# Odd feed-forward blocks take their low half from GpSimd, through a second relu copy by ScalarE

## What is computed

```python
x = x + jnp.tanh(g_xattn[0]) * _L0_xattn_ref(_layernorm(x), ctx, ctx, Wq, bq, Wk, bk, Wv, bv, Wo, bo)
x = x + jnp.tanh(g_ffn[0]) * _L0_ffn_ref(_layernorm(x), W1, b1, A1, B1, R1, W2, b2, A2, B2, R2)

# attention: 16 heads of 16, rotary positions with scale on q and k, softmax over the 154 rows
# feed-forward: both layers are
def _mole(x, W, b, A, Bm, Rw):          # 3 experts of rank 8
    gates = softmax(x @ Rw)
    base = x @ W + b
    z = einsum('bsd,edr->ebsr', x, A)
    zg = z * gates
    return base + (1/8) * einsum('ebsr,erh->bsh', zg, Bm)
h = relu(_mole(x, W1, ...))             # 256 -> 1024
return _mole(h, W2, ...)                # 1024 -> 256
```

## Time and profile before

| | |
|---|---|
| median of 3 runs | 569.35 us (567.44 to 569.93) |
| the profiled execution | 570.09 us, its span 568.3 us |
| mean granted TensorE clock | 0.953 |
| TensorE matmul busy | 505.9 us, 89% of the span |
| VectorE busy | 397.6 us, 70% |
| ScalarE busy | 208.7 us, 37% |
| GpSimd busy | 64.5 us, 11% |

### The profile page before, as it was taken

How to read it: one execution, slowest core, us unless ns; L and a number is a source line. 1 busy time by engine, 2 the same in 40 slices (tenths; PEclk the granted TensorE clock), 3 DMA queues, 4 the chain that set the end, 5 groups by cost and what they waited for, 6 DMA issues and landing times.

```text
span 568.3 us, 7827 instructions
## 1 busy us (share of the span) xinstructions
PE 505.9 (89%) x3032; PEld 375.8 (66%) x3032; DVE 397.6 (70%) x920; ACT 208.7 (37%) x341; POOL 64.5 (11%) x113
## 2 busy tenths in 40 slices
PE   2578865999999899999999999999999999999897
PEld 1345354855977387845977487746976497748697
DVE  4757465858879487958888487958887587925543
ACT  3233521363225612463326512463226413451230
POOL 2336002010110102010101002010201010010000
PEclk9965976999999999999999999999999999999898
DMA  8391044011802062112602171114502080200001
GB/s 294 49 226 39 1 81 68 2 50 45 106 0 76 8 114 30 40 49 66 84 0 77 38 99 14 50 39 82 69 1 76 1 112 1 77 1 1 1 38 37
DMA packets 13329, 31.86 MB, mean 56 GB/s; under 512 B 1732, under 2 KB 2572, under 8 KB 13164
## 3 DMA queue, kind: packets, MB, share of 16 engines
q1 hardware_dynamic: 6983, 14.63, 15.2%
q10 hardware_dynamic: 6309, 16.73, 11.0%
HBM read 14.31 MB, written 4.19 MB: 33 GB/s over the span
## 4 chain that ended last, share of the span: by engine, by line
PE 69%; DVE 16%; ACT 6%; DMA 5%; issue 3%; POOL 0%; SPq 0%; DVEq 0%; ACTq 0%
PE psF L1116 13%; PE psF L1164 13%; PE psX L1147 7%; PE psX L1218 5%; ACT probs L548 4%; DMA qT<-probs 4%; DVE max_t L762 4%; PE psX L1049 4%; PE psO L1232 3%; PE psO L1235 3%; PE psX L1032 2%; PE psF L1232 2%; DVE probs L687 2%; PE psF L1122 2%; PE psF L1235 2%
## 5 line engine op out<-in xcount | busy, mean ns | idle before, releaser
L762 DVE TENSOR_REDUCE max_t<-psX 128x4 fp32r<-128x616 f32 x128 | 99.2, 794 | 9.5 <-PE psX L1147 7.9
L548 ACT ACTIVATE probs<-psX 128x1024 f32<-128x1024 f32 x64 | 64.3, 1025 | 51.0 <-PE psX L1218 51.0
L1164 PE MATMUL psF<-w_hi,h_hi 128*128 128x284 f32 (+1 forms) x240 | 72.7, 303 | 0.0
L1147 PE MATMUL psX<-km,qT 96*128 96x308 f32 x256 | 64.7, 342 | 8.2 <-DMA qT<-probs 4.4
L1164 PE MATMUL psF<-w_lo,h_hi 128*128 128x284 f32 (+1 forms) x240 | 70.9, 296 | 0.0
L1164 PE MATMUL psF<-w_hi,h_lo 128*128 128x284 f32 (+1 forms) x240 | 70.8, 295 | 0.0
L1147 PEld LDWEIGHTS psX<-km,qT 96*128 96x128 f32 x256 | 48.2, 206 | 22.9 <-DVE max_t L762 9.7
L464 ACT ACTIVATE h_hi<-psF 128x512 fp32r<-128x512 f32 x59 | 34.3, 593 | 54.5 <-PE psF L1122 54.5
L1164 PEld LDWEIGHTS psF<-w_hi,h_hi 128*128 128x128 f32 x240 | 45.8, 191 | 4.9 <-issue 4.8
L1164 PEld LDWEIGHTS psF<-w_hi,h_lo 128*128 128x128 f32 x240 | 45.9, 191 | 0.1
L1164 PEld LDWEIGHTS psF<-w_lo,h_hi 128*128 128x128 f32 x240 | 45.7, 191 | 0.0
(11 more groups left out here) (175 smaller groups left out, 928.3 us busy)
## 6 DMA issues: line engine op xcount, KB each, us to landing
qT<-probs SPq DMA_DIRECT2D x32, 256.0 KB, 9.8
qT<-probs ACTq DMA_DIRECT2D x16, 256.0 KB, 8.1
x<-in_x_dram ACTq DMA_DIRECT2D x8, 512.0 KB, 3.3
x_ln<-in_x_dram ACTq DMA_DIRECT2D x7, 512.0 KB, 3.2
out_dram<-x ACTq DMA_DIRECT2D x7, 512.0 KB, 2.7
turn<-in_turns_dram SPq DMA_DIRECT2D x2, 512.0 KB, 10.1
heads_t<-in_w_dram SPq DMA_DIRECT2D x1, 1024.0 KB, 8.4
heads_t<-in_w_dram SPq DMA_DIRECT2D x1, 994.0 KB, 14.1
```

Of the source, the lines that this page charges most:

```text
L548: nc.scalar.activation(dst, psX[:, 2 * (i % 2):2 * (i % 2) + 2, :], ACT.Exp).then_inc(sc_exp.sem, 1)
L762: V.tensor_reduce(max_t[:, k, half, :].rearrange("p (h g) -> p g h", h=2)[:, 2 * j:2 * j + 2, :], psX[:, 2 * j:2 * j + 2, 0:2 * S].rearran ...
L1147: ins = mm(psX[:, g % 4, 0:2 * S], qT[0:KS, g, tokens(k)], km[0:KS, g, :, :].rearrange("p h s -> p (h s)"), start=True, stop=True)
L1164: ins = mm(out_bank(d, k)[:, cs], a[:, m, tokens(k)], w[:, m, cs], start=m == 0 and i == 0, stop=m == HT - 1 and i == 2)
```

## The change

For the odd blocks 1, 3, 5 and 7 of all chunks but the last, VectorE no longer forms the low half. ScalarE takes the relu of the same bank a second time, as exact fp32, into the first quarter, second quarter and so on of `heads_t` (named `h_f`, semaphore `w1_f`), and GpSimd subtracts: `h_lo = h_f - h_hi` (`low_blocks`, semaphore `w1_lo_p`). An odd block's bank is free when the second relu is done. VectorE's transposes of the next heads into `heads_t` wait for GpSimd's reads of the quarter that they overwrite. The first layer of the last chunk stays as it was.

```diff
@@ -210,7 +210,8 @@
         wo_ps, x1_s = count("wo_ps", 2), count("x1_s", 2)
         z1_ps, g1_v, g1_e = count("z1_ps", 1), count("g1_v", 9), count("g1_e", 1)
         z1T_ps, z1T_s = count("z1T_ps", 1), count("z1T_s", 1)
-        w1_ps, w1_hi_s, w1_lo_s = count("w1_ps", HT), count("h_hi_s", HT), count("h_lo_s", HT)
+        w1_ps, w1_hi_s = count("w1_ps", HT), count("h_hi_s", HT)
+        w1_lo_v, w1_lo_p, w1_f = (count(n, len(POOLED)) for n in ("h_lo_v", "h_lo_p", "h_f"))
         w2_ps = count("w2_ps", TT)
         g2_c, g2_v, g2_e = count("g2_c", TT), count("g2_v", 16), count("g2_e", 2)
         z2T_ps, z2T_s = count("z2T_ps", 2), count("z2T_s", 2)
@@ -248,6 +249,8 @@
                 return dict(out=lo, in0=staged[n][64:LR, :], in1=hi[64:LR, :].bitcast(F32), op=ALU.subtract)
             return dict(out=lo, in0=staged[n], in1=hi.bitcast(F32), op=ALU.subtract)
 
+        h_f = heads_t[:, :, :, :].rearrange("p a b c -> p a (b c)")
+
         block = stack.enter_context(nc.Block())
 
 
@@ -329,6 +332,13 @@
                 nc.gpsimd.tensor_tensor(ln_b[:, which, :], ln_n[:, which, :], ln_r[:, which, :],
                                         ALU.mult).then_inc(out_s.sem, 1)
 
+            def low_blocks(d):
+
+                for i, m in enumerate(POOLED):
+                    pool.wait_ge(w1_f.sem, w1_f.at(d, i + 1))
+                    nc.gpsimd.tensor_tensor(h_lo[:, m, :], h_f[:, i, :], h_hi[:, m, :].bitcast(F32),
+                                            ALU.subtract).then_inc(w1_lo_p.sem, 1)
+
             def residual_base(b, u):
 
                 pool.wait_ge(x1_loaded[u].sem, x1_loaded[u].at(b))
@@ -356,6 +366,8 @@
                 if first:
                     stage_low("w2a")
                     stage_low("w2b")
+                else:
+                    low_blocks(c - 1)
                 residual_base(b, u)
 
             rstd(0, ln1_agg, ln1_eps, ln1_rstd, 0)
@@ -462,6 +474,11 @@
 
                 act.wait_ge(w1_ps.sem, w1_ps.at(d, m + 1))
                 nc.scalar.activation(h_hi[:, m, :], hidden_bank(d, m), ACT.Relu).then_inc(w1_hi_s.sem, 1)
+                if m in POOLED and d is not LAST:
+                    i = POOLED.index(m)
+                    if i == 0:
+                        act.wait_ge(o_lo.sem, o_lo.at(d))
+                    nc.scalar.activation(h_f[:, i, :], hidden_bank(d, m), ACT.Relu).then_inc(w1_f.sem, 1)
 
             def maxima_copy(c):
 
@@ -754,7 +771,7 @@
                 dve.wait_ge(w1_hi_s.sem, w1_hi_s.at(d, m + 1))
                 V.scalar_tensor_tensor(out=h_lo[:, m, :], in0=hidden_bank(d, m), scalar=0.0,
                                        in1=h_hi[:, m, :].bitcast(F32), op0=ALU.max,
-                                       op1=ALU.subtract).then_inc(w1_lo_s.sem, 1)
+                                       op1=ALU.subtract).then_inc(w1_lo_v.sem, 1)
 
             def reduce_max(c, i):
                 half, k, j = i // 8, i % 8 // 2, i % 2
@@ -785,6 +802,8 @@
             def head_blocks(c, g):
 
                 dve.wait_ge(pv_ps.sem, pv_ps.at(c, g + 1))
+                if c:
+                    dve.wait_ge(w1_lo_p.sem, w1_lo_p.at(c - 1, g + 1))
                 V.transpose(heads_t[:, g, :, :].rearrange("p c r -> p (c r)"), pv_bank(g)).then_inc(pv_t.sem, 1)
 
             def head_norm(c, f2):
@@ -897,7 +916,8 @@
                     for m in range(HT):
                         if m < HT - 1:
                             reduce_max(c, 2 * m + 2)
-                        h_low(d, m)
+                        if m not in POOLED:
+                            h_low(d, m)
                         if m < HT - 1:
                             reduce_max(c, 2 * m + 3)
 
@@ -1010,7 +1030,7 @@
 
                 pe.wait_ge(ctx_loaded.sem, ctx_loaded.at(b))
                 if src is ctx_sb:
-                    pe.wait_ge(w1_lo_s.sem, w1_lo_s.at(2 * b - 2))
+                    block_taken(2 * b - 2, 7)
                 for f in range(FT):
                     nc.tensor.transpose(psF[:, 2, S * f:S * f + P], src[:, 0, P * f:P * f + P], ident)
                     ins = nc.tensor.transpose(psF[:, 2, S * f + P:S * f + S], src[0:SR, 1, P * f:P * f + P],
@@ -1096,6 +1116,15 @@
                     ins = nc.tensor.transpose(o_ps[:, k].bitcast(F32R), zs[:, k, :], ident_r[:, :])
                 ins.then_inc(z1T_ps.sem, 1)
 
+            def block_taken(d, m):
+
+                done = w1_f if m in POOLED else w1_lo_v
+                pe.wait_ge(done.sem, done.at(d, m // 2 + 1))
+
+            def lows_done(d):
+                pe.wait_ge(w1_lo_v.sem, w1_lo_v.at(d))
+                pe.wait_ge(w1_lo_p.sem, w1_lo_p.at(d))
+
             def hidden_main(d, m, second=False, parts=(0, 1)):
 
                 if d is LAST:
@@ -1104,10 +1133,10 @@
                     elif m == 6:
                         pe.wait_ge(g1_v.sem, g1_v.at(d, 1))
                     elif m == 7:
-                        pe.wait_ge(w1_lo_s.sem, w1_lo_s.at(d, 1))
+                        pe.wait_ge(w1_lo_v.sem, w1_lo_v.at(d, 1))
                 elif parts[0] == 0:
                     if m >= 3:
-                        pe.wait_ge(w1_lo_s.sem, w1_lo_s.at(d, m - 2))
+                        block_taken(d, m - 3)
                     elif not second:
                         pe.wait_ge(y_out.sem, y_out.at(d - 1, m + 2))
                 ops = [(a, w, f) for a, w in ((xT_hi, w1_hi), (xT_lo, w1_hi), (xT_hi, w1_lo)) for f in range(FT)]
@@ -1152,14 +1181,14 @@
 
                 if k == 0 and d is not LAST:
                     pe.wait_ge(w1_hi_s.sem, w1_hi_s.at(d))
-                    pe.wait_ge(w1_lo_s.sem, w1_lo_s.at(d))
+                    lows_done(d)
                 if k == 3 and m0 == 0 and d is not LAST and d is not LAST - 1:
                     pe.wait_ge(y_out.sem, y_out.at(d, 1))
                 cs = slice(0, E if k == 3 and d is LAST else W2N)
                 for m in range(m0, m1):
                     if k == 0 and d is LAST:
                         pe.wait_ge(w1_hi_s.sem, w1_hi_s.at(d, m + 1))
-                        pe.wait_ge(w1_lo_s.sem, w1_lo_s.at(d, max(m + 1, 2)))
+                        pe.wait_ge(w1_lo_v.sem, w1_lo_v.at(d, max(m + 1, 2)))
                     for i, (a, w) in enumerate(((h_hi, w2_hi), (h_lo, w2_hi), (h_hi, w2_lo))):
                         ins = mm(out_bank(d, k)[:, cs], a[:, m, tokens(k)], w[:, m, cs],
                                  start=m == 0 and i == 0, stop=m == HT - 1 and i == 2)
@@ -1305,7 +1334,8 @@
                         max_transposed(c, 1, first)
                     if i == 1 and not last:
                         if not first:
-                            pe.wait_ge(w1_lo_s.sem, w1_lo_s.at(d, 7))
+                            block_taken(d, 5)
+                            block_taken(d, 6)
                         transpose_x(c + 1, psF, ln1_out, xT_ps)
                     if i == 3 and u == 1 and not last:
                         ctx_transposed(b + 1, ctx_sb)
@@ -1377,6 +1407,7 @@
 PV_AFTER = [3, 5, 8, 10]
 PV_SLOT = {3: 0, 5: 1, 8: 2}
 LAST = B * UB - 1
+POOLED = (1, 3, 5, 7)
 QT_ACT = [0, 1, 2, 3, 4, 6]
 F_OF_K = [0, 1, 2, 0]
```

## The result

| | before | after |
|---|---|---|
| median (20 runs each) | 568.58 us (567.23 to 570.71) | 571.22 us (568.08 to 573.90) |
| ratio | | 1.0040, 95% interval 1.0023 to 1.0058 |
| profiled execution, span | 570.09, 568.3 us | 571.22, 569.4 us |

A forecast was written before the change was run, and what follows sets the result against it. TensorE was taken as the bound, with 69% of the chain; gain 0, GpSimd's price 0, and 0.35 us lost in each of six steps gave +2.1 us, median 571.4 us, range 568.5 to 575.0 us.

The forecast's parts named there:

- The forecast: Whole kernel: median of 571.4 us, 0.4% slower, from +2.1 us; given 45%.
- Nothing waits behind the odd low halves: Hidden blocks: removing VectorE's 28 instructions gains 0, at most 3.2 us.
- 0.48 us for the activation, not 0.60: Second relu of block 5, ahead of layer norm: delays relu 6 by 0.48 us; upper bound 0.60, full duration.
- Rival 3: Activation costs more than its spacing, or scores 1 and exponentials add waits: 0.47 to 0.59 us a step; chance 25%.
- 0.35 us a step: End of hidden blocks, steps 1 to 6: late relu 6 moves h_low(6) from 307.20 to 307.55, reduction 15 following.
- rival 2: Score part: reduction 15's delay is caught up there, no change, 569.4 us; chance 20%.
- Step 7 as before: Last step: no layer norm between relu 5 and relu 6, so relu 6 isn't late; nothing lost or won.
- GpSimd's price of 0: GpSimd's 28 added subtractions, 1.28 us each, 35.8 us in all, delay no reader: 0 us.
- The cover of 0.3 us in the last step: Last step: block 7's subtraction ends near 495.8, its reader starts at 496.09; covered by 0.3 us.
- The odd steps' first exponential: Odd steps: DMA issues behind two added activations delay the first exponential by some 0.4 us; third exponential still covered.
- the sum: Whole kernel: 6 x 0.35 = +2.1 us, on the profiled 570.09 us giving 572.2.
- VectorE's busy time: Whole kernel: falls by 19 us, from 28 removed instructions of 0.68 us.

The follow-up runs named there:

- block 5's copy alone: Kernel before plus one unread second relu of block 5 on ScalarE after relu 5 in steps 1 to 7, with waits for it; ratio 1.0012.
- the even blocks: Changed kernel with blocks 0, 2, 4 and 6 given to GpSimd in place of 1, 3, 5 and 7; ratio to before 0.9958.

## Why the prediction was right

- **The forecast**: 0.4% slower, +2.1 us; measured 1.0040, +2.3 us. That the two lie this close is partly luck, since the interval runs from +1.3 to +3.3 us; the steps carry the cause. The mechanism is shown from both sides: block 5's copy alone makes the loss, moving it behind relu 7 takes the loss away.
- **Nothing waits behind the odd low halves**: taken as 0, and the kernel that leaves them out measured 0.
- **0.48 us for the activation, not 0.60**: relu 6 moved from 2.46 to 2.94. The second relu of a bank follows the first at 0.49 us (305.62, 306.11). Rival 3 was out. The budget in the Trainium skill's page "ScalarE: Activation LUTs", section "Rules for kernel authors", which the page gives for an activation whose bias is a pointer operand, comes to an estimated 0.72 us; the trace doesn't agree, with 0.48 to 0.49 us from one activation to the next.
- **0.35 us a step**: 0.35 to 0.39. This is 0.48 less the 0.13 us by which relu 6 had been early for `h_low(6)`. It went through the score part undiminished; rival 2, that it would be caught up there, had 20% and was wrong.
- **Step 7 as before**: 61.00 against 61.01.
- **GpSimd's price of 0**: right. The cover of 0.3 us in the last step was 0.24 by the rows after, some 0.1 of it really spare, since the prediction counted nothing for the handover from GpSimd to TensorE (0.14 us).
- **The odd steps' first exponential**: forecast to slip by some 0.4 us behind the DMA issues, and it didn't move (4.57 us after relu 5). The prediction put the issues behind the added activations; they run beside them, and ended 4.01 us after relu 5 in step 5, before 4.00. The slip was said to be covered, so the sum did not suffer.
- **What was off**: the sum was built on one profiled execution of 570.09 us, and the profile after came out 1.1 us above it, not 2.1, since the clock gave the two executions different first and last stretches. VectorE's busy time fell by 13.5 us and not by 19. The larger miss came later, in the forecast for the even blocks, and is named there.

## What to carry to other kernels

An engine that is 96% busy in a stretch is not its bound while the engine it serves has no idle time behind the instructions one means to take off; ask for each instruction who is queued behind it. An instruction added to an engine that is 37% busy is paid for where that engine happens to work through without a pause, here in front of a layer norm behind which relu 6 is queued: 0.48 us at relu 6, 0.35 us of it in the step. And before work is moved to another engine, the order in the list is worth a look: setting one reduction ahead of one low half gave 1.2 us, where moving four low halves lost 2.

## What the runs showed of the hardware

A ScalarE activation of 128x512 whose row lasts 0.59 to 0.60 us takes 0.48 to 0.49 us of a full queue, also when two in a row read the same PSUM bank. GpSimd's fp32 subtraction of 128x512 takes 1.286 us and held up neither VectorE's reductions from PSUM nor its subtractions with one operand in SBUF. The issue of a DMA on ScalarE's queue ran beside its activations (370.33 to 370.76, with relu 7 from 370.17 to 370.76). TensorE's first product behind a wait for GpSimd started 0.14 us after the subtraction ended. The clock granted to TensorE in the first 100 us and in the tail differed between executions (0.93 and 0.96 in the tail), which moves a span by more than 1 us: to tell 2 us in 570, the distances between steps at full clock were a better measure than ratios of five rounds.
